# Multi-head maxima of two heads in two matmuls with padded keys; routing positions and gates in eight steps between latent maxima

## The chip, the cores and the metric

The kernel runs on one core of a Trainium2 chip. The metric is the device time of one execution in microseconds (us). The engines are named PE (TensorE), DVE (VectorE), ACT (ScalarE), POOL (GpSimd) and SP (SyncE, which issues most DMAs).

## What is computed

Eight sequences (B = 8) of 256 tokens with 256 channels go through two branches and come together at the end:

```python
xn = _layernorm(x)
s = latent_attention(xn)        # 16 heads, 64 rotary + 16 other dimensions, causal softmax
h = multi_head_attention(rms(xn, w_ln1))   # 16 heads of 16 dimensions, causal softmax
y = xn + h @ Wo.T
f = y + moe(rms(y, w_ln2))      # 8 experts, top 2 of a router, gates = softmax of the two logits
out = x + s * silu(f)
```

All arithmetic is float32. To come close to it on PE, operands are split into a high part, rounded to float32r (a rounded float32 that PE multiplies in one pass), and the rest; a float32 matmul is run in two passes. The softmax needs each row's maximum before the exponential, and both attentions take it in a matmul of their own.

## The kernel before

**The loop.** `batch(b, first, more)` exists once for each engine and is called for b = 0 to 7; each engine runs its own list of work in order, and semaphores tie the lists together. A batch has four stages on PE. *P2* transposes the maxima of the latent scores and then, in eight units of four 128x128 transposes, the multi-head queries (even units) and keys (odd units) of the batch (`stage_p2`, L716). *T1* computes the transposed latent scores head by head (`scores1`), from which ACT takes exponentials, POOL masks them (`causal`), and PE multiplies them with the values four heads at a time (`values(g)`). After each head `max_head` issues the raw scores of the multi-head attention (`max2`), whose row maxima DVE takes (`stage_m2`, `maxima`, L1397 and L1400). *P1* projects the next batch (`stage_p1`), while DVE and POOL apply the rotary terms. *T2* is T1 with the roles changed: transposed multi-head scores (`scores2`) and, between them, the raw latent scores of the next batch (`max1`), whose maxima DVE takes in `stage_m1`.

**An order written by hand.** Other work is hung between the heads with dictionaries `after`, from the index of a head to a function. On DVE in T1: after head 4 the residual sum of the batch behind (`kept`, xn, L1342), after 5 its statistics, after 7 the copy of the next batch's x (`copy_batch`), after 9 the scaled rows for the router, after 12 the low part of the next x. The router's top two (`top_two`) follow the last head, and its last instruction (`ohb`, L1516) releases PE's second projection of P1, as both use the bank `ps[1]`. In T2: splits of the next batch's queries and keys after 3, 5, 7, 12 and 14, rounding of queries (`rounded`) before the even heads, `positions` of the batch behind after head 1 and `gates` after head 4. On PE in T1: transposes of the batch behind's normalised heads after head 0 (`back`, L621), its output projection after 3, the transposes of the next x after 10 (L645), the router's transposes after 11 and logits after 14. `values(0)` waits for the residual sum (x2d).

**Maxima before.** Two heads share the 128 partitions: `kt2` holds keys in pairs, `qt2` holds the queries of each head alone, with zeros in the other head's 64 partitions. For each head PE multiplies 128 queries with 128 keys and the other 128 queries with all 256 keys, into bank `ps[2 + h % 2]`; it waits until DVE is done with head h - 2. The even heads' halves of the query units are cut by ACT, the odd ones' by DVE (`odd_heads`, L1237), three of them ahead of the normalisation (`normalise`, L1322 and L1327) and one behind it.

**Positions, gates and scatters.** For the tokens of the batch behind, DVE computes their row in each chosen expert's list and the gate values, in chains of small instructions of which each waits for the one before (semaphores pst and gst). The last one signals posd, on which POOL's four indirect DMAs (`scatter_slot`, L515) wait. POOL runs them after its masks of heads 9 to 12 of T2 (`slots_between`); the masks of the next heads stand behind them in its queue, and `values(g)` waits for the masks of its heads.

## Time and profile before

| | us |
|---|---|
| median of 3 runs | 956.92 (955.44 to 962.53) |
| the profiled execution, its time | 958.59 |
| its span, from first to last instruction | 956.9 |

| engine | busy us | share | instructions |
|---|---|---|---|
| PE matmuls | 830.5 | 87% | 6432 |
| PE weight loads | 743.6 | 78% | 6432 |
| DVE | 625.2 | 65% | 2207 |
| ACT | 501.6 | 52% | 1089 |
| POOL | 392.2 | 41% | 538 |

The chain of work that ended last is 67% PE, 10% DVE and 9% DMA. The batches run up to about 660 us; then come the experts. The mean granted clock of PE is 0.935 of 2.4 GHz. Busy times of PE are modelled and overlap: a matmul's start to the start of the next is what it costs in a stream. A row of the timeline may merge several instructions of one kind, with their number (x4); the shape shown is then the first one's.

### The profile page before, as it was taken

Reading aid. Unit: us, or ns where it says so; the run is one execution under the profiler, and the core shown is the slowest. Engines: PE = TensorE matmul, PEld = TensorE weight load, DVE = VectorE, ACT = ScalarE, POOL = GpSimd, SP = SyncE. Lnnn points to the kernel's source line nnn. Section 1 sums busy time; section 2 is a strip of 40 time slices with the busy share of each in tenths; the row PEclk is TensorE's granted clock in tenths of the full one; section 3 lists DMA queues with packets and bytes.
Section 4 is the critical chain, followed back from the end, with each engine's and each line's share of the span. In section 5 each row is a group of like instructions: output and inputs, shape, how many; then the busy total and the mean of one; then the engine's idle time right before and its main releaser. Section 6 shows DMA issues by size and latency. Waiting matters only on the chain.

```text
span 956.9 us, 18123 instructions
## 1 busy us (share of the span) xinstructions
PE 830.5 (87%) x6432; PEld 743.6 (78%) x6432; DVE 625.2 (65%) x2207; ACT 501.6 (52%) x1089; POOL 392.2 (41%) x538
## 2 busy tenths in 40 slices
PE   5889999999999999999998998965269999998980
PEld 3868978978887887887897897843169999998980
DVE  4876677667677667757758757632257777776754
ACT  3445375366366456456356446540146677776651
POOL 5522432343343334344344344331404756555541
PEclk9878999999999999999999999976579999999995
DMA  8000000000000000000000000030236776889736
GB/s 273 1 1 2 13 1 25 12 2 13 24 1 14 13 13 2 24 12 3 23 13 2 24 12 3 23 144 23 47 134 176 221 220 198 238 240 348 193 53 186
DMA packets 39884, 71.04 MB, mean 74 GB/s; under 512 B 10914, under 2 KB 34850, under 8 KB 36834
## 3 DMA queue, kind: packets, MB, share of 16 engines
q1 hardware_dynamic: 29074, 57.39, 17.6%
q0 software_dynamic: 9856, 12.13, 6.7%
q8 instruction: 52, 0.85, 0.4%
q10 hardware_dynamic: 864, 0.36, 0.2%
q14 instruction: 38, 0.31, 0.1%
HBM read 55.12 MB, written 14.81 MB: 73 GB/s over the span
## 4 chain that ended last, share of the span: by engine, by line
PE 67%; DVE 10%; DMA 9%; issue 6%; POOL 2%; ACT 2%; SPq 2%; POOLq 0%; DVEq 0%; ACTq 0%
PE ps L586 54%; DMA expert_rows<-yo,slot_of 6%; PE ps L679 6%; PE ps L716 3%; DVE ps L1400 2%; PE ps L612 2%; DVE ps L1397 1%; SPq L425 1%; PE ps L621 1%; DVE qr L1237 1%; DMA w_ukv_raw<-in_w_ukv 1%; DMA raw<-in_w_experts 1%; SPq L441 1%; POOL slots L515 1%; POOL expert_rows L563 1%
## 5 line engine op out<-in xcount | busy, mean ns | idle before, releaser
L523 POOL TENSOR_SCALAR_AFFINE_SELECT ex<-ex 128x256 f32<-128x256 f32 x256 | 107.6, 425 | 246.5 <-ACT ex L1101 245.1
L1101 ACT ACTIVATE ex<-ps 128x384 f32<-128x384 f32 x256 | 125.4, 497 | 118.9 <-PE ps L586 116.8
L586 PE MATMUL ps<-qt,kt 128*128 128x256 f32 (+1 forms) x768 | 164.1, 325 | 8.6 <-ACT ex L1101 4.6
L502 POOL TENSOR_TENSOR tok<-tok,swp 128x256 f32<-128x256 f32 x128 | 97.4, 761 | 114.7 <-DVE swp L1362 113.7
L1397 DVE CUSTOM_DVE_ANT_0 ps<-ps,mask 128x128 f32<-128x128 f32 x256 | 77.4, 302 | 94.9 <-PE ps L586 90.5
L586 PEld LDWEIGHTS ps<-qt,kt 128*128 128x128 f32 x768 | 108.9, 193 | 20.7 <-issue 9.8
L563 POOL DMA_INDIRECT expert_rows<-yo,slot_of x46 | 78.5, 1707 | 110.8 <-DMA expert_rows<-yo,slot_of 55.6
L1400 DVE CUSTOM_DVE_ANT_0 ps<-ps,mask 128x256 f32<-128x256 f32 x256 | 118.9, 465 | 0.0
L1241 DVE TENSOR_TENSOR wel<-raw,weh 128x768 fp32r<-128x768 f32 x92 | 88.4, 961 | 37.2 <-ACT weh L971 36.0
L586 PE MATMUL ps<-wh,xth 128*128 128x320 f32 (+2 forms) x352 | 96.9, 358 | 3.7 <-DVE wl L1241 2.8
L1358 DVE TENSOR_TENSOR tok<-ps,cos_t 128x320 f32<-128x320 f32 x128 | 62.9, 491 | 52.8 <-PE ps L586 52.2
L586 PE MATMUL ps<-xeh,weh 128*128 128x256 f32 x368 | 79.4, 298 | 11.8 <-issue 9.9
L971 ACT ACTIVATE qt<-ps 128x512 f32<-128x512 f32 (+1 forms) x96 | 57.2, 596 | 61.9 <-PE ps L679 59.8
L971 ACT ACTIVATE kt<-ps 128x512 f32<-128x512 f32 (+1 forms) x96 | 57.4, 598 | 53.4 <-PE ps L679 48.3
L586 PE MATMUL ps<-wh,xtl 128*128 128x320 f32 (+2 forms) x352 | 84.1, 321 | 0.0
L586 PE MATMUL ps<-wl,xth 128*128 128x320 f32 (+2 forms) x352 | 83.8, 320 | 0.0
L971 ACT ACTIVATE weh<-raw 128x768 fp32r<-128x768 f32 x92 | 77.9, 846 | 10.1 <-DMA raw<-in_w_experts 10.1
L679 PE MATMUL ps<-idf,tok 128*128 128x128 f32 x512 | 77.0, 273 | 0.0
L586 PE MATMUL ps<-xeh,wel 128*128 128x256 f32 x368 | 75.9, 289 | 0.0
L586 PE MATMUL ps<-xel,weh 128*128 128x256 f32 x368 | 75.8, 288 | 0.0
L586 PE MATMUL ps<-kt,qt 128*128 128x128 f32 (+1 forms) x256 | 73.4, 368 | 0.0
L586 PE MATMUL ps<-kr,qr 128*128 128x128 f32 (+1 forms) x256 | 58.6, 316 | 16.8 <-DVE negm L1400 13.1
(160 smaller groups left out, 1918.3 us busy)
## 6 DMA issues: line engine op xcount, KB each, us to landing
raw<-in_w_experts SPq DMA_DIRECT2D x23, 1536.0 KB
mla_branch<-s_b SPq DMA_DIRECT2D x8, 256.0 KB, 2.1
expert_rows<-xn SPq DMA_DIRECT2D x8, 256.0 KB, 2.2
x_normalised<-otk SPq DMA_DIRECT2D x8, 256.0 KB, 2.1
xr<-in_x SPq DMA_DIRECT2D x1, 2048.0 KB
s_tok<-mla_branch SPq DMA_DIRECT2D x1, 2048.0 KB
w_cols_raw<-in_w_cols SPq DMA_DIRECT2D x1, 1792.0 KB, 15.4
x<-expert_rows SPq DMA_DIRECT2D x3, 512.0 KB, 5.2
```

What stands on the lines that cost most here:

```text
L502: nc.gpsimd.tensor_tensor(t, t, swp[:, n % 2, :, :], ALU.add).then_inc(tokd, 1)
L523: nc.gpsimd.affine_select(a, a, [[0, 2], [1, P]], ALU.is_ge, zero, 0, -1).then_inc(exm, 1)
L563: nc.gpsimd.indirect_dma_start(ys[:, :], bass.IndirectOffsetOnAxis(mt_b[:, blk, j, 1:2], 0), yo[:, blk % 2, j, :], None, compute_op=ALU.ad ...
L586: return nc.tensor.matmul(o, a, m, start=start, stop=stop, skip_group_check=True, **k)
L679: t = nc.tensor.transpose(ps[2 + n % 2][:, j * P:(j + 1) * P], tok[:, n % 4, j, :], idf[:, :])
L716: i = nc.tensor.transpose(bank2(u)[:, j * P:(j + 1) * P], a[:, p0:p0 + P], idf[:, :])
L971: return nc.scalar.activation(o, a, ACT.Copy)
L1101: nc.scalar.activation(ex[:, h % (2 * G), :], ps[4 + h % 2][:, P:4 * P], ACT.Exp, scale=scale).then_inc(ex_, 1)
L1241: return nc.vector.tensor_tensor(o, a, b.bitcast(F32), ALU.subtract)
L1358: nc.vector.tensor_tensor(tok[:, n % 4, :, 0:HW], a, cos_t[:, tt:tt + 1, :].broadcast_to([P, G, HW]), ALU.mult)
L1397: nc.vector.tensor_tensor_reduce(out=o[:, 0:P], in0=o[:, 0:P], in1=mask2[:, 1, :], scale=-1.0, scalar=-2.0 * BIG, op0=ALU.add, op1=ALU.min ...
L1400: nc.vector.tensor_tensor_reduce(out=o[:, S:2 * S], in0=o[:, S:2 * S], in1=mask2[:, :, :].rearrange("p a k -> p (a k)"), scale=-1.0, scala ...
```

## The change

`qt2` now holds queries in pairs and `kt2` the keys of each head alone, padded with zeros. A pair of heads has its maxima in two matmuls: 128 queries against the first 128 keys of both heads (256 columns, bank `ps[3]`), and the other 128 queries against all keys of both (512 columns, bank `ps[2]`). PE issues them after every second head, each one when DVE is done with the same bank of the pair before. DVE takes two maxima of 128 columns, then two of 256; a function hung after index 4 now runs after the first half of pair 2. The odd halves are cut from the key units instead of the query units. `scores2` takes the padded keys as weights; its shapes are the same. `positions` and `gates` are cut into eight steps; in batches 1 to 6 they are hung after the latent maxima of heads 1, 2, 4, 6, 8 (two steps), 9 and 10, and elsewhere they run as before. The four scatters move from behind the masks of heads 9 to 12 to behind those of heads 11 to 14, the last batch's too. The memory cleared by POOL is now that of `kt2`.

```diff
@@ -173,8 +173,8 @@
         mask2 = sb("mask2", [P, 2, P], BF16, late)
         wo1 = sb("wo1", [P, ET, E], F32, late)
         wo2 = sb("wo2", [P, ET, E], F32, late)
-        qt2 = sb("qt2", [P, H, S], F32R, late)
-        kt2 = sb("kt2", [P, H // 2, S], F32R, late)
+        qt2 = sb("qt2", [P, H // 2, S], F32R, late)
+        kt2 = sb("kt2", [P, H, S], F32R, late)
         v2 = sb("v2", [P, 2, H, PADV], F32, late)
         ex = sb("ex", [P, 2 * G, 3 * P], F32, late)
         ov = sb("ov", [P, NG, S], F32, late)
...
@@ -385,7 +385,7 @@
                 sp.wait_ge(mte2, b + 1)
                 for e in range(2):
                     r = ST * e + MROW2
-                    sp.dma_start(qt2[r:r + 1, e:H:2, :].bitcast(F32),
+                    sp.dma_start(qt2[r:r + 1, :, :].bitcast(F32),
                                  mt[e * H // 2:(e + 1) * H // 2, :]).then_inc(md2, 16)
 
...
@@ -524,7 +524,7 @@
                     after.get(h, lambda: None)()
 
             def slots_between(r):
-                return {9 + 2 * t + k: lambda t=t, k=k: scatter_slot(r, t, k) for t in range(2) for k in range(2)}
+                return {11 + 2 * t + k: lambda t=t, k=k: scatter_slot(r, t, k) for t in range(2) for k in range(2)}
 
             zero = nc.gpsimd.to_reg(0.0)
@@ -708,7 +708,7 @@
                     if u >= 3:
 
                         wait(pe, t2e, 8 * b + u - 2)
-                        if (u - 3) % 2 == 0:
+                        if (u - 3) % 2 == 1:
                             wait(pe, t2o, 4 * b + (u - 3) // 2 + 1)
                     a = (qs, ks)[u % 2][:, u // 4, :, :].rearrange("p h c -> p (h c)").bitcast(F32)
                     for j in range(4):
@@ -737,12 +737,20 @@
 
             def max2(b):
                 def head(h):
-                    if h == 0:
+                    if h % 2 == 0:
+                        return
+                    j = h // 2
+                    if j == 0:
                         wait(pe, t2e, 8 * b + 8)
                         wait(pe, t2o, 4 * b + 4)
-                    if h >= 2:
-                        wait(pe, mx2, 16 * b + h - 1)
-                    raw_scores(ps[2 + h % 2], qt2[:, h, :], kt2[:, h // 2, :]).then_inc(m2d, 1)
+                    else:
+                        wait(pe, mx2, 16 * b + 2 * j - 1)
+                    mm(ps[3][:, 0:2 * P].rearrange("p (e k) -> p e k", e=2), qt2[:, j, 0:P],
+                       kt2[:, 2 * j:2 * j + 2, 0:P], True, True).then_inc(m2d, 1)
+                    if j > 0:
+                        wait(pe, mx2, 16 * b + 2 * j)
+                    mm(ps[2][:, :].rearrange("p (e k) -> p e k", e=2), qt2[:, j, P:S],
+                       kt2[:, 2 * j:2 * j + 2, :], True, True).then_inc(m2d, 1)
                 return head
 
@@ -782,8 +790,8 @@
                 return mm(o[:, 2 * P:4 * P], kt[:, h, 0:P], qt[:, h, :], True, True)
 
             def scores2(h, o):
-                mm(o[:, 0:2 * P], kt2[:, h // 2, P:S], qt2[:, h, :], True, True)
-                return mm(o[:, 2 * P:4 * P], kt2[:, h // 2, 0:P], qt2[:, h, :], True, True)
+                mm(o[:, 0:2 * P], kt2[:, h, P:S], qt2[:, h // 2, :], True, True)
+                return mm(o[:, 2 * P:4 * P], kt2[:, h, 0:P], qt2[:, h // 2, :], True, True)
 
             def stage_t1(b, after):
@@ -1075,11 +1083,11 @@
                     t = slice(u // 4 * P, (u // 4 + 1) * P)
                     a = bank2(u)[:, :].rearrange("p (h t) -> p h t", h=4)
                     if u % 2 == 0:
+                        copy(qt2[:, 4 * (u // 2 % 2):4 * (u // 2 % 2) + 4, t], a).then_inc(t2e, 1)
+                    else:
 
                         h0 = 8 * (u // 2 % 2)
-                        copy(qt2[0:ST, h0:h0 + 8:2, t], a[0:ST, :, :]).then_inc(t2e, 1)
-                    else:
-                        copy(kt2[:, 4 * (u // 2 % 2):4 * (u // 2 % 2) + 4, t], a).then_inc(t2e, 1)
+                        copy(kt2[0:ST, h0:h0 + 8:2, t], a[0:ST, :, :]).then_inc(t2e, 1)
                     after.get(u, lambda: None)()
 
@@ -1387,9 +1395,18 @@
 
             def stage_m2(b, after):
                 wait(dve, mtr2, b)
-                for h in range(H):
-                    maxima(b, h, (h % 2) * (H // 2) + h // 2, negm2, m2d, mx2)
-                    after.get(h, lambda: None)()
+                for j in range(H // 2):
+                    for t in range(2):
+                        wait(dve, m2d, 16 * b + 2 * j + t + 1)
+                        n = (t + 1) * P
+                        for e in range(2):
+                            o = ps[3 - t][:, e * n:(e + 1) * n]
+                            col = e * (H // 2) + j
+                            i = nc.vector.tensor_tensor_reduce(
+                                out=o, in0=o, in1=mask2[:, 1 - t:2, :].rearrange("p a k -> p (a k)"), scale=-1.0,
+                                scalar=-2.0 * BIG, op0=ALU.add, op1=ALU.min, accum_out=negm2[:, t, col:col + 1])
+                        i.then_inc(mx2, 1)
+                        after.get(2 * j + t, lambda: None)()
 
@@ -1419,11 +1436,11 @@
 
             def odd_heads(b, i):
 
-                wait(dve, tr2, 8 * b + 2 * i + 1)
+                wait(dve, tr2, 8 * b + 2 * i + 2)
                 t = slice(i // 2 * P, (i // 2 + 1) * P)
                 h0 = 8 * (i % 2)
-                copy(qt2[ST:P, h0 + 1:h0 + 8:2, t],
-                     bank2(2 * i)[ST:P, :].rearrange("p (h t) -> p h t", h=4)).then_inc(t2o, 1)
+                copy(kt2[ST:P, h0 + 1:h0 + 8:2, t],
+                     bank2(2 * i + 1)[ST:P, :].rearrange("p (h t) -> p h t", h=4)).then_inc(t2o, 1)
 
@@ -1451,8 +1468,10 @@
                                      14: lambda: rounded(b + 1, 1)})
                     after = splits(b + 1)
                     if not first:
-                        after[1] = lambda: positions(b - 1)
-                        after[4] = lambda: gates(b - 1)
+                        in_expert, chosen, summed, kept, stepped = position_steps(b - 1)
+                        plus_one, inverse, both = gate_steps(b - 1)
+                        after |= {1: in_expert, 2: chosen, 4: summed, 6: kept, 8: lambda: (stepped(), plus_one()),
+                                  9: inverse, 10: both}
                     stage_m1(b + 1, after)
...
+            def position_steps(r):
+
+                def in_expert():
+                    dve.wait_ge(rnk, r + 1)
+                    nc.vector.tensor_tensor(pose[:, :, :], ps[1][:, 0:2 * NE].rearrange("p (t e) -> p t e", t=2),
+                                            base[:, :].unsqueeze(1).broadcast_to([P, 2, NE]), ALU.add).then_inc(pst, 1)
+
+                def chosen():
+                    dve.wait_ge(pst, 6 * r + 2)
+                    nc.vector.tensor_tensor(base[:, :], ps[1][:, 2 * NE:3 * NE], base[:, :], ALU.add).then_inc(pst, 1)
+                    for t in range(2):
+                        i = nc.vector.tensor_tensor(posx[:, t, :, :], oh[:, t, :, :],
+                                                    pose[:, t:t + 1, :].broadcast_to([P, 2, NE]), ALU.mult)
+                    i.then_inc(pst, 1)
+
+                def summed():
+                    dve.wait_ge(pst, 6 * r + 4)
+                    nc.vector.tensor_reduce(posf[:, :, :].rearrange("p t k -> p (t k)"),
+                                            posx[:, :, :, :].rearrange("p t k e -> p (t k) e"), AX.X,
+                                            ALU.add).then_inc(pst, 1)
+
+                def kept():
+                    dve.wait_ge(pst, 6 * r + 5)
+                    wait(dve, msc, 64 * r)
+                    copy(posu[:, :, :], posf[:, :, :])
+                    ids = rc[:, C_IDS:C_IDS + 8].rearrange("p (t k f) -> p t k f", t=2, k=2)
+                    for t in range(2):
+                        i = copy(meta[:, t, :, 0:2], ids[:, t, :, :])
+                    i.then_inc(pst, 1)
+
+                def stepped():
+                    dve.wait_ge(pst, 6 * r + 6)
+                    step = rc[:, C_IDS:C_IDS + 8].rearrange("p (a f) -> p a f", f=2)
+                    nc.vector.tensor_scalar(step[:, :, :], step[:, :, :], 2.0 * P, None, ALU.add).then_inc(gst, 1)
+                return in_expert, chosen, summed, kept, stepped
+
+            def gate_steps(r):
+                g = meta[:, :, :, 2].bitcast(F32)
+
+                def plus_one():
+                    dve.wait_ge(gex, r + 1)
+                    nc.vector.tensor_scalar(gsum[:, :], gexp[:, :], 1.0, None, ALU.add).then_inc(gst, 1)
+
+                def inverse():
+                    dve.wait_ge(gst, 3 * r + 2)
+                    nc.vector.reciprocal(gsum[:, :], gsum[:, :]).then_inc(gst, 1)
+
+                def both():
+                    dve.wait_ge(gst, 3 * r + 3)
+                    copy(g[:, :, 0], gsum[:, :])
+                    nc.vector.tensor_tensor(g[:, :, 1], gexp[:, :], gsum[:, :], ALU.mult).then_inc(posd, 1)
+                return plus_one, inverse, both
+
             def positions(r):
...
```

## Rows read from the trace of the kernel before

**Rows 1.** Windows, four stages of a batch: stretch, length, busy us, granted clock, DMA

```profile
core 0: us, PE busy (x) PEld busy (x) DVE busy (x) ACT busy (x) POOL busy (x), PEclk, DMA share, GB/s
370.20:375.00 4.80, 4.79 (x42) 4.50 (x43) 2.60 (x6) 3.71 (x9) 0.00 (x0) 1.00 0.03 7
375.00:396.50 21.50, 21.27 (x174) 18.37 (x173) 15.08 (x75) 11.42 (x26) 7.25 (x17) 1.00 0.08 26
396.50:425.00 28.50, 28.36 (x219) 26.88 (x218) 17.38 (x53) 12.00 (x23) 11.95 (x16) 1.00 0.04 12
425.00:444.70 19.70, 16.90 (x154) 12.80 (x151) 16.75 (x91) 13.03 (x32) 10.84 (x20) 1.00 0.01 1
```

**Rows 2.** Timeline of PE in T1: start, us, tiles, shapes, count, idle before

```profile
377.05 0.82 PE L586 MATMUL ps<-qt,kt 128*128 128x128 f32 x4
...
377.93 0.82 PE L586 MATMUL ps<-qt,kt 128*128 128x128 f32 x4
```

**Rows 3.** Timeline of PE in T2: scores and maxima, then a projection

```profile
432.23 0.39 PE L586 MATMUL ps<-kr,qr 128*128 128x128 f32 x2
432.46 0.40 PE L586 MATMUL ps<-qt,kt 128*128 128x256 f32 x2
432.69 0.39 PE L586 MATMUL ps<-kr,qr 128*128 128x128 f32 x2
...
436.31 0.63 PE L586 MATMUL ps<-wl,xth 128*128 128x512 f32 x2
436.77 0.63 PE L586 MATMUL ps<-wh,xtl 128*128 128x512 f32 x2
```

**Rows 4.** Timeline from P2 into T1

```profile
374.12 0.60 PE L716 MATMUL ps<-idf,qs 128*128 128x128 f32 x4
...
374.57 0.63 PE L716 MATMUL ps<-idf,ks 128*128 128x128 f32 x4
...
375.67 0.42 PEld L621 LDWEIGHTS ps<-idf,otk 128*128 128x128 f32 x4 [0.22 <-DVE otk L1327]
```

**Rows 5.** Timeline of T1, heads 4 to 6

```profile
382.51 0.30 DVE L1397 CUSTOM_DVE_ANT_0 ps<-ps,mask 128x128 f32<-128x128 f32 x1
...
382.72 0.47 DVE L1400 CUSTOM_DVE_ANT_0 ps<-ps,mask 128x256 f32<-128x256 f32 x1
...
383.10 0.69 DVE L1342 TENSOR_TENSOR xn<-ps,xn 128x512 f32<-128x512 f32 x1
...
384.17 0.59 PEld L586 LDWEIGHTS ps<-ex,v 128*32 128x32 f32 x16
```

**Rows 6.** Timeline at the start of P1, second projection

```profile
398.86 0.30 PEld L586 LDWEIGHTS ps<-wh,xth 128*128 128x128 f32 x2 [0.43 <-DVE ohb L1516]
```

**Rows 7.** Timeline of DVE and PE in the front of T2

```profile
427.79 0.17 DVE L1521 TENSOR_TENSOR pose<-ps,base 128x16 f32<-128x16 f32 x1
...
429.10 0.41 DVE L1237 CAST qr<-qt 128x512 fp32r<-128x512 f32 x1
...
430.31 0.47 PE L586 MATMUL ps<-kr,qr 128*128 128x128 f32 x2 [1.12 <-DVE negm L1400]
```

**Rows 8.** Timeline of POOL, ACT and PE at the end of T2

```profile
439.73 0.98 POOL L515 DMA_INDIRECT slots<-meta,posu  x1 [0.17 <-issue]
...
441.35 0.98 POOL L515 DMA_INDIRECT slots<-meta,posu  x1 [0.17 <-issue]
442.35 1.13 POOL L523 TENSOR_SCALAR_AFFINE_SELECT ex<-ex 128x256 f32<-128x256 f32 x3
...
437.67 0.49 ACT L1101 ACTIVATE ex<-ps 128x384 f32<-128x384 f32 x1 [0.76 <-PE ps L586]
...
443.53 0.86 PE L586 MATMUL ps<-ex,v 128*32 128x256 f32 x16
444.72 0.39 PE L602 MATMUL ps<-idf,negm 128*16 128x128 f32 x2 [0.34 <-DVE negm L1400]
```

**Rows 9.** Windows around a fall of the granted clock, T2 of another batch

```profile
350.73:354.15 3.42, 2.15 (x13) 1.49 (x12) 3.28 (x23) 3.23 (x9) 1.91 (x5) 1.00 0.00 0
354.15:357.56 3.41, 3.30 (x15) 3.33 (x16) 2.35 (x15) 0.00 (x0) 0.29 (x1) 0.50 0.03 5
```

38 lines of the change are left out of this document (6 added, 32 removed).

## The prediction

> **What bounds the kernel now.** I read the page first: TensorE (PE) is busy most of the span, and two thirds of the chain that ended last is PE. So any PE time that is saved counts, and so does any new wait in PE's in-order queue. Then I cut one batch of the steady state into its four stages and took the windows of each [rows 1]: 4.8 us of transposes (P2), 21.5 us of latent scores with the multi-head maxima between them (T1), 28.5 us of projections (P1), 19.7 us of multi-head scores with the latent maxima (T2). T1 and P1 are PE-bound (21.27 of 21.50 us busy). T2 is not (16.90 of 19.70): there PE, VectorE (DVE) and GpSimd (POOL) wait for each other. A batch is 74.5 us, and six of the eight (1 to 6) are alike; the figures below are for one of these.
>
> **The maxima on PE.** In T1 a head of latent scores and a head of maxima together take 0.88 us from start to start [rows 2]. The old maxima of a head (128 columns, then 256) take 0.23 us, exactly what two matmuls of 256 columns take; in both cases 0.115 us each, so 128 columns cost as much as 256 [rows 3]. A matmul of 512 columns of the same kind takes 0.23 us: two of them 0.46 us. So a pair of heads cost 4 x 0.115 = 0.46 us and will cost 0.115 + 0.23 = 0.35 us: 0.11 us saved per pair, 0.9 us per batch, 7 us in all if PE never waits. Scores alone are 0.88 - 0.23 = 0.65 us. The price of the new forms is the least certain in the first term: nothing saved (0.46) at one end, 0.33 at the other.
>
> The Trainium skill (TensorE: Matmul & The Clock Gate, "Back-to-back issue gap") gives N/2.4 + 2.5 ns for an isolated matmul: 56, 109 and 216 ns for 128, 256 and 512 columns, so 330 ns a pair before and 325 after. The trace disagrees in the first of these: 115 ns for the 128 columns. By the rule the change saves PE nothing.
>
> **What becomes late because of it.** DVE needs 0.21 us from the start of a 128-column maximum to the next instruction and 0.38 us for a 256-column one [rows 5]: 0.6 us a head, 1.2 us a pair, far below PE's 1.65 us. But both heads now wait for one issue, behind the scores of the next head, and what DVE does between maxima waits with them. I walk PE through P2 and T1.
> (a) P2. The odd halves are now cut from keys, whose transposes come one unit after the queries'. A unit is 0.45 us of PE [rows 4]. DVE's third odd copy stands ahead of the normalisation (reciprocals, two products), and PE's weights for the transposes of its result already waited 0.22 us for it [rows 4]. So these come 0.45 us later, and head 1 with them: +0.46 us.
> (b) The residual sum of the batch behind (xn, 0.69 us) runs after the first maxima of pair 2 instead of after head 4. DVE began head 4's maxima at 382.51 [rows 5], 0.43 after their issue (0.23 of matmul, 0.2 of passing on), so the scores of head 6 ended one head later, at 382.96. Pair 2 is issued there: +0.46 - 5 x 0.23 + 2 x 0.35 = +0.01, at 382.97. Then 0.12 of matmul, 0.2 to DVE, 2 x 0.21, 0.69 for xn, 0.05 back: 384.45. The first values wait for xn; they started at 384.17 [rows 5], and PE would be there at 384.0. So +0.3 us instead of -0.1.
> (c) Pair 3 and the batch copy behind it slip the same way (statistics, 1.34 us, stand between): the transposes of the next x start some 0.6 us late, and half of that is regained up to head 12. At head 13 I have +0.47. The router's logits wait for a ScalarE copy that follows head 13, so pair 6 gains nothing.
> (d) End of T1. The last issue comes 0.23 us earlier (head 14's maxima are no longer before the values), but DVE then has 2 x 0.21 + 2 x 0.38 = 1.20 us to do behind it, not 0.60, less 0.12 since it starts after one matmul: +0.25. PE already waits there for the marked experts that follow the maxima [rows 6], so it lands in full: +0.7 us at the start of P1. P1 is PE-bound and carries it on.
>
> **Positions and gates.** Eight steps spread over T2. Before, the positions held DVE from 427.79 to 429.10: 1.31 us between two maxima, mostly one small instruction waiting for the one before; PE stood idle 1.12 us for the maxima behind them [rows 7]. Now one step (0.08 us) stands there, so the next maxima come 1.2 us earlier and PE with them. The other steps (about 0.08 us each when nothing is waited for, 10 instructions) are added where DVE was continuously busy, heads 6 to 9: -0.2. At head 11 I have -1.05 us. The gates cost nothing before (PE was in a projection) and 0.25 us now, in that sum.
>
> **The scatters behind them.** They are ready only after head 10, so the four scatters move on POOL from behind the masks of heads 9 to 12 to behind those of heads 11 to 14. A mask is 0.42 us, a scatter 0.98 us, from one scatter to the next with the mask and the gaps 1.62 us [rows 8]. Before, the last mask ended at 443.48 and the values of the last group started at once (443.53); only 0.34 us of slack lay between them and the next stage, which waited for DVE [rows 8]. Now: exp of head 11 ends at 438.16 - 1.05 = 437.1, its mask at 437.6, first scatter 437.8 to 438.8; the mask of head 12 at 439.06 (its exp binds), then three times 1.62 and a mask: 444.35. The last values start at 444.4, 0.88 us, P2 at 445.28 instead of 444.72: **+0.56 us** where the shorter DVE chain alone would have given -1. What is queued behind the masks on POOL is only the next batch's; what waits for them is PE, and with it everything.
>
> **The clock.** In three of the six batches (one is shown, the two others look the same) the granted clock fell to 0.50 (1.2 GHz) for 3.4 us after the front of T2; in the 3.42 us before, PE had 13 matmuls and 2.15 us busy [rows 9]. I take a fall there at 1.5 us: 3.3 us of PE work at half clock, less what was waiting anyway. The front gets denser, so I take these off: -4.5 us. But PE now stands idle some 2.5 us before the last values (last maxima done near 441.8, values at 444.4), a thinner stretch than the one shown. I expect falls there in four to six batches, each doubling the values and transposes after it for part of the time: 1.3 us each, +6.5. Net +2, bounds -4.5 (no fall) and +5.
>
> **Sum.** Batches 1 to 6: 6 x (0.7 + 0.56) = +7.6. Batch 0 has no residual sum, router or scatters: -0.6. The last batch: T1 +0.7, and its scatters, in a T2 where POOL is busy throughout, +0.3. Together +8.0, with the clock +10. The profiled execution has a span of 956.9 us in a time of 958.6; its span happens to equal the median, so the forecast is 956.9 + 10 = **967 us**.
>
> **Rivals.**
> 1. *Slower by waits and POOL, as worked out:* 962 to 974 us, with the clock deciding where. Chance 0.62.
> 2. *The same waits, but no falls of the clock at the end of T2, or half of the slips taken up by slack I did not see:* 3 to 4 us over, 957 to 962. For it: PE's waits in T1 are each only 0.3 to 0.5 us. Chance 0.22.
> 3. *Faster: the scatters do not hold PE.* It decides at a scatter's hold on POOL of under about 0.65 us; then P2 comes 1 us earlier: 6 x (0.7 - 1.0) - 0.6 + 0.7 - 4.5 = -6, 951 us. Against it: all four are 0.98 to 1.03 us, and the old last mask already ended 0.06 us before its values. Chance 0.07.
> 4. *PE saves nothing by the wider matmuls* (512 columns dearer than in the projections, 0.46 us a pair): +0.11 x 6 pairs more per batch, about 972 us. Chance 0.05.
> 5. *The clock, once fallen at the end of T2, stays low through P2,* whose 42 matmuls are nearly all transposes. At half clock a transpose takes twice its 0.11 us, so 4.4 us per batch: 8 - 4.5 + 26, near 987 us. Against it: P2 shows a clock of 1.00 throughout [rows 1]. Chance 0.04.
>
> Rival 5 is what the Trainium skill says (same page, "PE-mode transpose"): transposes don't count as busy in the same way and don't bring the full clock. By that rule P2 should have lost it; the trace does not agree so far, but shows no P2 that began low.
>
> **Numbers.** Changes of 1% (9.6 us, the bounds 947.4 and 966.5) are about what a measurement of this kernel can tell from none. Slower by over 1%: most of the upper half of rival 1, rivals 4 and 5: 0.47. Within: lower half of rival 1, rival 2: 0.47. Faster: part of rival 3: 0.06. The range 956 to 974 leaves out rivals 3 and 5.
>
> **What would show it.** Right: two matmuls in place of four, in 0.35 us a pair, in T1; idle on PE before its transposes of the normalised heads and before the first values, naming xn; no 1.1 us idle for the maxima in the front of T2; the last mask about 0.9 us later than before counted from the stage's start, and PE's last values released by POOL after over 2 us idle; the clock at 0.50 in several P2 stages. Wrong: P2 starting under 19.7 us after T2's start, or T1 under 21.5 us.

## The result, and the profile after

| | before | after |
|---|---|---|
| median of four runs each, same chip, us | 956.18 (954.51 to 962.53) | 975.2 (970.45 to 976.21) |
| the profiled execution, us | 958.59 | 975.67 |
| its span, us | 956.9 | 973.9 |
| mean granted clock | 0.935 | 0.935 |

The changed kernel takes 1.0177 times as long (95% interval 1.0119 to 1.0234), 17 us more by this ratio and by the two spans (the medians stand 19 us apart). It is slower, on the side that was forecast, and 8 us beyond the single number.

Windows of the kernel after. The first three are P2, T1 and P1 of a steady batch, the fourth a T2 without a fall of the clock (another batch), the last two the stretch before the end of a T2 and the one after it. They answer to [rows 1, 9]; as there, the windows part T1 from P1 at the first projection.

```profile
core 0: us, PE busy (x) PEld busy (x) DVE busy (x) ACT busy (x) POOL busy (x), PEclk, DMA share, GB/s
453.17:458.05 4.88, 4.81 (x46) 4.53 (x43) 2.08 (x3) 3.95 (x9) 0.00 (x0) 1.00 0.04 7
458.05:480.30 22.25, 21.08 (x158) 16.68 (x157) 14.75 (x74) 11.58 (x26) 7.25 (x17) 1.00 0.07 25
480.30:509.10 28.80, 28.27 (x217) 26.74 (x216) 17.99 (x57) 11.79 (x23) 11.94 (x16) 1.00 0.03 11
587.10:607.47 20.37, 17.10 (x154) 12.90 (x153) 16.29 (x91) 12.76 (x31) 10.96 (x20) 1.00 0.02 2
527.00:529.00 2.00, 0.26 (x7) 0.17 (x10) 0.80 (x5) 0.00 (x0) 1.50 (x3) 1.00 0.03 2
529.00:532.40 3.40, 3.40 (x28) 2.72 (x21) 0.00 (x0) 1.35 (x3) 0.00 (x0) 0.50 0.02 4
```

P2 takes 4.88 us for 4.80, T1 22.25 for 21.50, P1 28.80 for 28.50, T2 20.37 for 19.70. PE's busy time fell in T1 (21.08 for 21.27), but its idle time rose by more. The last two rows are the fall that the forecast looked for: 0.26 us of PE in the 2 us before, then 3.4 us at 0.50, and 1.00 again behind it.

Timeline of PE in T1, in the start of P1 and at the end of a T2, kernel after (start, us, engine, line, operation, tiles, shapes, count, idle before it and what ended that). It answers to [rows 4, 5, 6, 8].

```profile
459.29 0.66 PE L621 MATMUL ps<-idf,otk 128*128 128x128 f32 x4 [0.41 <-DVE otk L1335]
...
467.77 0.86 PE L586 MATMUL ps<-ex,v 128*32 128x256 f32 x16 [0.39 <-DVE xn L1350]
...
477.33 1.06 PE L586 MATMUL ps<-wr,s_b 128*128 128x8 f32 x8 [0.27 <-ACT s_b L979]
...
483.00 0.56 PE L586 MATMUL ps<-wh,xth 128*128 128x320 f32 x2 [0.53 <-DVE ohb L1535]
...
513.41 0.47 PE L586 MATMUL ps<-kr,qr 128*128 128x128 f32 x2
...
528.75 1.32 PE L586 MATMUL ps<-ex,v 128*32 128x256 f32 x16 [2.57 <-POOL ex L523]
530.00 0.59 PE L602 MATMUL ps<-idf,negm 128*16 128x128 f32 x2
```

The longest waits of PE are ones that the forecast had named: its transposes of the normalised heads (0.41 us for DVE's product), the first values (0.39 us for xn), the second projection of P1 (0.53 us behind the transposes, for ohb), and 2.57 us for POOL before the last values, where the kernel before had its masks done in time [rows 8]. The 1.12 us of idle time in the front of T2 [rows 7] are gone; the matmul that stood behind them starts at 513.41 without a wait. The next P2 begins at 530.00, although DVE was done with the last latent maxima at 527.8. DVE's rows of the first step (pose), of the last (meta) and of the last maxima, same T2, with [rows 7, 8] of before:

```profile
511.93 0.17 DVE L1541 TENSOR_TENSOR pose<-ps,base 128x16 f32<-128x16 f32 x1
...
521.90 0.16 DVE L1587 TENSOR_TENSOR meta<-gexp,gsum 128x2 f32<-128x2 f32 x1
...
527.67 0.13 DVE L1417 DVE_READ_ACCUMULATOR2_ANT negm<- 128x1 f32 x1
```

The last step, which signals posd, ends at 522.1. POOL, same T2:

```profile
522.34 1.03 POOL L515 DMA_INDIRECT slots<-meta,posu  x1 [0.38 <-DVE meta L1587]
...
524.13 0.97 POOL L515 DMA_INDIRECT slots<-meta,posu  x1 [0.17 <-issue]
...
527.28 0.97 POOL L515 DMA_INDIRECT slots<-meta,posu  x1 [0.17 <-issue]
528.28 0.41 POOL L523 TENSOR_SCALAR_AFFINE_SELECT ex<-ex 128x256 f32<-128x256 f32 x1
```

Each scatter waits behind a mask and each mask behind a scatter, 1.57 to 1.79 us apart. The last mask ends at 528.7, 19.57 us after T2's start at 509.12; before, it was 18.49 us (443.48 - 424.99).

**Where the 17 us are.** The table adds up stages from the starts of PE's instructions (P2 begins with the transposes of the latent maxima, T1 with the first latent score, P1 here with the transposes of the multi-head maxima, 1.8 us later than in the windows, T2 with the first multi-head score). Each value is that of a batch without a fall in the stage or running into it; batches 1 to 6 agree within 0.03 us, but for one T2 of the kernel before (20.11).

| us | P2 | T1 | P1 | T2 |
|---|---|---|---|---|
| before | 4.82 | 23.31 | 26.65 | 19.74 |
| after | 4.88 | 24.01 | 27.06 | 20.36 |

That is 1.79 us a batch, 10.7 us in six. From the start of batch 1's P2 to that of batch 7's it is 452.5 us before and 464.3 after, 11.8 more; so the falls in between cost 1.1 us more than before. The last batch adds 4.9 us: 1.7 in a P2 with a fall, 1.3 in T1, 1.9 in T2 (up to the transposes of its values). Batch 0 and what is ahead of it add 0.1, the experts 0.2.

### The profile page after: what moved, and what is told of

It is laid out like the page before. It is cut to its first block, busy times and chain, and to the rows that moved or that the text cites. A ratio compares the mean times of both kernels' runs of the same rounds, so it can differ in the third digit from the quotient of the medians.

```text
span 973.9 us, 17859 instructions
## 1 busy us (share of the span) xinstructions
PE 831.5 (85%) x6304; PEld 730.8 (75%) x6304; DVE 619.4 (64%) x2207; ACT 501.1 (51%) x1089; POOL 393.6 (40%) x538
## 4 chain that ended last, share of the span: by engine, by line
PE 55%; DMA 14%; issue 11%; DVE 8%; POOL 7%; ACT 4%; SPq 0%; POOLq 0%; ACTq 0%; DVEq 0%
PE ps L586 42%; DMA expert_rows<-yo,slot_of 11%; PE ps L679 6%; POOL slots L515 3%; PE ps L716 3%; PE ps L612 2%; ACT ex L1109 1%; POOL ex L523 1%; POOL expert_rows L563 1%; DVE ps L1405 1%; PE ps L621 1%; POOL xg L552 1%; DMA w_ukv_raw<-in_w_ukv 1%; DMA xg<-x_normalised,slot_of 1%; DVE otk L1335 1%
## 5 line engine op out<-in xcount | busy, mean ns | idle before, releaser
L586 PE MATMUL ps<-qt,kt 128*128 128x256 f32 (+1 forms) x768 | 159.1, 326 | 6.0 <-issue 3.2
L586 PEld LDWEIGHTS ps<-qt,kt 128*128 128x128 f32 x768 | 113.6, 193 | 21.0 <-ACT ex L1109 7.6
L1405 DVE CUSTOM_DVE_ANT_0 ps<-ps,mask 128x128 f32<-128x128 f32 (+1 forms) x256 | 85.0, 384 | 57.1 <-PE ps L586 57.0
L586 PE MATMUL ps<-xeh,weh 128*128 128x256 f32 x368 | 78.6, 296 | 11.8 <-issue 9.8
L586 PE MATMUL ps<-ex,v 128*32 128x256 f32 (+1 forms) x1024 | 57.5, 344 | 22.5 <-POOL ex L523 19.8
L1196 ACT ACTIVATE sg<-ps 128x256 f32<-128x256 f32 x92 | 35.7, 388 | 69.3 <-PE ps L586 66.6
L586 PEld LDWEIGHTS ps<-xeh,weh 128*128 128x128 f32 x368 | 57.9, 195 | 15.8 <-issue 15.8
```

Of the source, the lines that this page charges most:

```text
L586: return nc.tensor.matmul(o, a, m, start=start, stop=stop, skip_group_check=True, **k)
L1196: nc.scalar.activation(sg[:, n % 2, :], ps[n % 3][:, 0:BS], ACT.Silu).then_inc(sgd, 1)
L1405: i = nc.vector.tensor_tensor_reduce(out=o, in0=o, in1=mask2[:, 1 - t:2, :].rearrange("p a k -> p (a k)"), scale=-1.0, scalar=-2.0 * BIG, ...
```

## The experiments

There are twelve runs of ten kernels, on four chips; every ratio is against the kernel before on the same chip. Stages are read as in the table above. The part of a run from the last batch's last values on (mostly the experts) took between 301.9 and 307.2 us in the profiled executions, with no relation to the edits, so that stages tell more than spans do.

### Each half alone

The first kernel has the eight steps and the new places of the scatters, nothing of the pairs (the functions of the steps, as in the change, are left out here):

```diff
-                return {9 + 2 * t + k: lambda t=t, k=k: scatter_slot(r, t, k) for t in range(2) for k in range(2)}
+                return {11 + 2 * t + k: lambda t=t, k=k: scatter_slot(r, t, k) for t in range(2) for k in range(2)}
...
-                        after[1] = lambda: positions(b - 1)
-                        after[4] = lambda: gates(b - 1)
+                        in_expert, chosen, summed, kept, stepped = position_steps(b - 1)
+                        plus_one, inverse, both = gate_steps(b - 1)
+                        after |= {1: in_expert, 2: chosen, 4: summed, 6: kept, 8: lambda: (stepped(), plus_one()),
+                                  9: inverse, 10: both}
```

> The kernel before with the second half of the change alone: positions and gates in eight steps, scatters behind the masks of heads 11 to 14; the maxima stay one head at a time. Theory (the two halves cost about the same, and this one costs through GpSimd): the front of T2 gets its 1.05 us back, but the last mask ends with the scatters, so that T2 of batches 1 to 6 is some 0.6 us longer than before when the clock is full, 6 x 0.6 = 3.6 us, the last batch 1.9 (what the changed kernel shows), and the falls of the clock move from the front of T2 to its end, +2.7: 965 us, PE idle over 2 us for POOL before the last values. Rival (T2 became longer because of the padded keys or the order of the maxima, not by the scatters): this kernel has no cause to be slower, and wins 1.05 us per batch and the three falls in front: 945 to 957 us.

Measured: 963.56 us, ratio 1.0113 (1.0076 to 1.0150). Window of a T2 without a fall, and PE's last values in it:

```profile
428.67:449.04 20.37, 17.09 (x154) 12.91 (x153) 16.28 (x91) 12.77 (x31) 10.96 (x20) 1.00 0.01 1
```

```profile
448.25 0.86 PE L586 MATMUL ps<-ex,v 128*32 128x256 f32 x16 [2.58 <-POOL ex L523]
```

T2 is 20.37 us as in the whole change, T1 and P1 are those of the kernel before (23.30 and 26.65). Falls came at the end of T2 or the start of the next P2 in five of the batches 1 to 6, none in the front of T2. So the longer T2 belongs to this half alone, and POOL ends it (2.58 us of idle PE). The profiled span was 960.1 us, 5 below the expectation: the part behind the batches took 4.3 us less than in the kernel before, and the last batch's T2 grew by 0.7 us, not 1.9.

The second has the pairs and nothing of the steps:

```diff
-                    raw_scores(ps[2 + h % 2], qt2[:, h, :], kt2[:, h // 2, :]).then_inc(m2d, 1)
+                    mm(ps[3][:, 0:2 * P].rearrange("p (e k) -> p e k", e=2), qt2[:, j, 0:P],
+                       kt2[:, 2 * j:2 * j + 2, 0:P], True, True).then_inc(m2d, 1)
+                    if j > 0:
+                        wait(pe, mx2, 16 * b + 2 * j)
+                    mm(ps[2][:, :].rearrange("p (e k) -> p e k", e=2), qt2[:, j, P:S],
+                       kt2[:, 2 * j:2 * j + 2, :], True, True).then_inc(m2d, 1)
```

> The kernel before with the first half alone: maxima of two heads in two matmuls, odd halves cut from keys; positions, gates and scatters as before. Theory: PE starts the second projection of P1 1.1 us later per batch than before (+0.7 in T1, +0.4 behind it), 6 x 1.15 = 7 us, the last batch 1.3, batch 0 0.2: about 965 us, with T2 and its falls of the clock as before (19.74 us without a fall). Rival (the delay in T1 comes from what the second half leaves behind, falls of the clock at the end of T2 and transposes at a low clock): T1 23.3 us and no more than 958 us.

Measured: 959.99 us, ratio 1.0058 (1.0031 to 1.0085); its profiled span 965.3 us. T1 24.01, P1 27.04, and T2 as before, with the three falls in its front, as before. The window of a T2 without a fall, and PE's second projection of P1:

```profile
505.00:524.68 19.68, 16.87 (x155) 12.84 (x152) 16.90 (x91) 12.76 (x31) 10.60 (x20) 1.00 0.01 2
```

```profile
403.21 0.56 PE L586 MATMUL ps<-wh,xth 128*128 128x320 f32 x2 [0.53 <-DVE ohb L1533]
```

The same 0.53 us for ohb as in the whole change. So the two halves hit different stages, and their ratios multiply to that of the whole (1.0113 x 1.0058 = 1.0172). The stages of the rival stated with this run did not appear: this half costs its 1.1 us a batch without any fall at the end of T2.

### Do the scatters hold T2, and does their wait let the clock fall?

```diff
             def slots_between(r):
-                return {11 + 2 * t + k: lambda t=t, k=k: scatter_slot(r, t, k) for t in range(2) for k in range(2)}
+                return {H - 1: lambda: [scatter_slot(r, t, k) for t in range(2) for k in range(2)]}
```

> The changed kernel with all four scatters behind the mask of head 15, where POOL has nothing to do until the first mask of the next T1 some 6 us later. Theory (the last values wait for POOL's masks, which stand behind the scatters, and the clock falls in this wait): the last mask follows its exponential at about 17.4 us of T2, the last values start there, and the next P2 waits only for the last latent maxima, which end at 527.8 where P2 now starts at 530.0: 2.1 us less in each of six batches, 1.5 in the last, and no fall of the clock at the end of T2 (8.2 us): 973.9 - 12.6 - 1.5 - 8.2 = 951.6 us of span. Rival (the falls at the end of T2 come from its thin stretch whatever waits there, since PE still waits a little for the masks): the falls stay and only the waits go, about 960 us. Rival (the maxima on DVE set the end of T2, and the scatters just fill the time): under 3 us, 970 us or more.

Measured: 943.24 us, ratio 0.9904 (0.9866 to 0.9942), span 941.6. Windows of P2 and of T2:

```profile
438.20:443.09 4.89, 4.82 (x43) 4.54 (x44) 2.08 (x3) 3.69 (x9) 2.37 (x3) 1.00 0.04 5
494.16:512.39 18.23, 17.07 (x154) 12.88 (x152) 15.83 (x91) 13.13 (x32) 8.37 (x18) 1.00 0.01 1
```

```profile
512.39 0.39 PE L602 MATMUL ps<-idf,negm 128*16 128x128 f32 x2 [0.45 <-DVE negm L1417]
```

T2 fell from 20.36 to 18.23 us, and PE's last wait is again 0.45 us for DVE. Not one fall of the clock is left in batches 1 to 6, neither in the front of T2 nor at its end. From batch 1's P2 to batch 7's it is 445.3 us, for 464.3: 19.0 less, of which 12.8 are waits and the rest falls. So the scatters set the end of T2, and without the 2.6 us of idle PE there was no fall. The span is 10 us below the 951.6 expected: 1.9 of these lie ahead of batch 1, 4.7 behind the batches and 3.5 in the last T2, where the clock was low for a shorter time; the steady batches came as expected. The changed kernel with its scatters out of the way is 1% faster than the kernel before.

The same edit on the kernel before, positions whole:

```diff
-                return {9 + 2 * t + k: lambda t=t, k=k: scatter_slot(r, t, k) for t in range(2) for k in range(2)}
+                return {H - 1: lambda: [scatter_slot(r, t, k) for t in range(2) for k in range(2)]}
```

> The kernel before with one edit: all four scatters behind the mask of head 15 (positions and gates whole, maxima one head at a time). Theory (in the kernel before two things end T2 at nearly the same time, POOL's masks and DVE's latent maxima, which positions held up for 1.3 us in front): taking away the one alone gives next to nothing, T2 without a fall stays at 19.6 to 19.74 us, the falls in the front of T2 stay, 953 to 957 us of span. Rival (the scatters alone bound T2, and the eight steps are worth nothing): T2 at 18.2 us, 6 x 1.5 = 9 us less, 948 us.

Measured: 967.24 us, ratio 1.0102 (1.0061 to 1.0142). Window of the one T2 without a fall, and PE's wait in its front:

```profile
430.64:449.72 19.08, 16.85 (x154) 12.82 (x151) 16.19 (x91) 12.78 (x31) 8.38 (x18) 1.00 0.01 1
```

```profile
435.95 0.47 PE L586 MATMUL ps<-kr,qr 128*128 128x128 f32 x2 [1.11 <-DVE negm L1400]
```

The 1.11 us for the maxima behind the positions are there as in [rows 7]. In the five other batches the clock fell in the front of T2, which then takes 20.65 to 21.05 us; without a fall it is 19.08, by this one batch. Neither the theory (19.6 to 19.74) nor the rival (18.2) had this: of the 1.5 us between 19.74 and 18.23, 0.65 come from the scatters alone, with the positions' hold still there, and 0.85 more with the steps. That the kernel became slower, and not only no faster, is another matter: all its P2 from batch 2 on took 6.7 to 8.1 us, the two longest with a fall of the clock in them. This was not expected, and came in all four kernels that ran on that chip.

### A stall in P2 that depends on the chip or the run

This kernel is the one with the eight steps and without the pairs, and the same line for the scatters.

> The kernel before with positions and gates in eight steps and the scatters behind the mask of head 15; maxima one head at a time. Against the 941.6 us of the changed kernel with the scatters there it differs only in the maxima. Theory (pairs cost 1.1 us per batch at the end of T1 and the start of P1, as maxima alone showed, and save nothing elsewhere): 941.6 - 6 x 1.1 - 1.3 = 934 us, T2 of 18.2 us and no fall of the clock in batches 1 to 6. Rival (with T2 short, the thinner T2 and the denser T1 change where the clock falls): falls in T2 or P2 come back, 1.3 us each, 940 us.

Measured: 953.16 us, ratio 0.9936 (0.9907 to 0.9965). T1 23.30, P1 26.65, T2 18.25 and no fall in batches 1 to 6, all as in the theory, but P2 7.25 us. ACT and PE there (the last copy of values and what follows it):

```profile
442.09 0.38 ACT L971 ACTIVATE ov<-ps 128x256 f32<-128x256 f32 x1 [1.22 <-PE ps L586]
445.14 0.38 ACT L971 ACTIVATE ov<-ps 128x256 f32<-128x256 f32 x1 [2.66 <-remote]
```

```profile
442.06 0.86 PE L586 MATMUL ps<-ex,v 128*32 128x256 f32 x16
...
445.57 1.09 PE L612 MATMUL ps<-idf,ov 128*128 128x128 f32 x8 [1.39 <-issue]
```

PE issued the last values at 442.06, and the copy that waits for them alone began at 445.14, 2.66 us of idle ACT whose end the trace puts down to nothing of this core (remote), while POOL issued its four scatters. In the changed kernel with the scatters last the copy came 0.9 us after the values' issue. ACT is not alone in this: DVE's first odd copy began 3.8 us after PE had issued the transposes that it reads (443.58 to 447.38), and 0.7 us after them in the second run of this kernel below (436.17 to 436.87). So what came late is PE's side of the hand-over, its work or its signals, and not ACT. To see whether kernel or chip makes the difference, both ran again elsewhere:

> The same kernel as the changed one with the scatters last, measured once more beside the two below, because the four kernels with the scatters there that ran on another chip all had a P2 of 6.7 to 7.3 us at full clock, where this one had 4.9: ScalarE's last copy of the values, released by PE's last values, came 2.2 us late. Theory A (four scatters in a row hold up PE's last values as PE's own semaphores show it, and whether they do depends on the chip or the run): here P2 is 6.8 us in at least some batches and the time lies between 943 and 957 us. Theory B (it depends on the kernel's own timing, and this kernel is free of it): P2 is 4.9 us again and the time 943 us.

Measured: 946.73 us, ratio 0.9896 (0.9870 to 0.9923), P2 4.89 (in batches 2 and 3 of both its runs 5.28 to 5.66, most of which T1 made up).

> The kernel before with positions and gates in eight steps and the scatters behind the mask of head 15, once more. In its first run each P2 of batches 2 to 7 held ScalarE's last copy of the values back by 2.2 us and took 6.8 to 7.3 us; the changed kernel with the same scatters has not shown this on two other chips. Theory A (it hangs on the chip or the run): on another chip P2 is 4.8 us in batches 2 to 7 and the span 951.3 - 6 x 2.4 = 937 us. Theory B (it hangs on the kernel: when its last values meet the scatters): P2 is 6.8 to 7.3 us again and the span 951 us.

Measured: 935.95 us, ratio 0.9783 (0.9755 to 0.9811), span 936.9, P2 4.82 but for batch 2 (5.50). The same copy of ACT:

```profile
435.57 0.38 ACT L971 ACTIVATE ov<-ps 128x256 f32<-128x256 f32 x1 [0.84 <-PE ps L586]
```

The same kernel has the stall on one chip and none on another, so theory A holds for it. What makes it is open; no run here separates chip from run. For the comparison it leaves a clean pair, on different chips: with the scatters last and no stall, maxima one head at a time take 935.95 us (ratio 0.978) and pairs 943 to 947 us (0.990 both times). The pairs by themselves cost some 8 us by the stages, 6 x 1.1 and 1.3 in the last T1, and 1.2% by the ratios.

### Why the pairs cost what they do

```diff
                         for e in range(2):
                             o = ps[3 - t][:, e * n:(e + 1) * n]
                             col = e * (H // 2) + j
+                            if t == 1:
+                                o = o[:, P:2 * P]
                             i = nc.vector.tensor_tensor_reduce(
-                                out=o, in0=o, in1=mask2[:, 1 - t:2, :].rearrange("p a k -> p (a k)"), scale=-1.0,
+                                out=o, in0=o, in1=mask2[:, 1, :], scale=-1.0,
```

> The changed kernel, with the 256-column maxima of the second half of a pair taken over their last 128 columns only (so the maximum subtracted is that of the diagonal block): two instructions of 0.21 us in place of two of 0.38 us. It takes 0.34 us of DVE from each pair and nothing from PE. In the changed kernel a pair costs PE 0.40 to 0.48 us where 0.35 was expected: in batch 0 the pairs start at 81.75, 83.52 and 85.21 us, 1.77 and 1.69 us apart, of which two heads of scores are 1.31. Theory (PE's second matmul of a pair waits until DVE is done with the pair before, as its weights are loaded only then): the pairs stand 1.66 us apart, batch 0's T1 is some 0.5 us shorter (18.75 us), and ohb comes 0.7 to 0.9 us earlier in each of batches 1 to 6. Rival (the matmul of 512 columns, or of two strided blocks, is dearer by itself): the distances stay 1.70 or more and batch 0's T1 stays at 19.2 us; only the 0.34 us at the end of T1 are won, about 2 us in all.

Measured: 969.85 us in one run (the kernel before on the same chip: 954.76), so that only its trace is read here. Pairs of batch 0 in T1, first the changed kernel (PE, then its weight loads, then DVE), then the one with short maxima (PE):

```profile
82.29 1.58 PE L586 MATMUL ps<-qt,kt 128*128 128x128 f32 x8
...
84.08 1.47 PE L586 MATMUL ps<-qt,kt 128*128 128x128 f32 x8
...
85.79 0.38 PE L586 MATMUL ps<-qt,kt 128*128 128x128 f32 x2
```

```profile
82.94 0.52 PEld L586 LDWEIGHTS ps<-qt,kt 128*128 128x128 f32 x4 [0.24 <-ACT ex L1109]
```

```profile
82.26 0.30 DVE L1405 CUSTOM_DVE_ANT_0 ps<-ps,mask 128x128 f32<-128x128 f32 x1 [1.58 <-PE ps L586]
...
83.55 0.14 DVE L1405 DVE_READ_ACCUMULATOR2_ANT negm<- 128x1 f32 x1
84.02 0.30 DVE L1405 CUSTOM_DVE_ANT_0 ps<-ps,mask 128x128 f32<-128x128 f32 x1 [0.33 <-PE ps L586]
```

```profile
81.88 1.58 PE L586 MATMUL ps<-qt,kt 128*128 128x128 f32 x8
...
83.64 1.47 PE L586 MATMUL ps<-qt,kt 128*128 128x128 f32 x8
...
85.31 0.82 PE L586 MATMUL ps<-qt,kt 128*128 128x128 f32 x4
```

From one pair of scores to the next it is 1.79 and 1.71 us, and with short maxima 1.76 and 1.67; less two heads of scores (1.31) the second of each is 0.40 and 0.36. In the first, a weight load also waits 0.24 us for ACT's exponential, as two heads of scores now come without maxima between them. DVE begins 0.5 us after the pair's first matmul is issued and needs 1.4 us for its four maxima (82.26 to 83.69), and PE's next second matmul needs that bank: the loop is as long as PE's own. Batch 0's T1 is 18.78 us, the theory's 18.75, against 19.24 in the changed kernel and 19.29 before. So of the 0.9 us that eight pairs should save there, DVE's part of the loop takes 0.46, as this run shows, and 0.05 are left; the rest goes with the wait for the exponentials, which no run took away. In batches 1 to 6 T1 and P1 are 0.27 us shorter each, 0.54 of the 0.7 expected.

### The waits in T1 taken away one by one

```diff
-                odd_heads(b, 2)
                 normalise()
+                odd_heads(b, 2)
                 odd_heads(b, 3)
-                after = {4: kept}
+                after = {1: kept}
                 if not first:
                     after[5] = lambda: stats_x2(b - 1)
                     after[9] = lambda: scale_x2(b - 1)
+                    after[13] = lambda: top_two(b - 1)
...
                 stage_m2(b, after)
-                if not first:
-                    top_two(b - 1)
```

The first of these kernels has only the lines on `top_two`, the second all; both have the scatters last.

> The changed kernel with the scatters last and the router's top two hung behind the second half of pair 6 instead of behind the last pair: they need the logits, which PE finishes near 478.4 us, and DVE sits idle from 478.7 to 480.3. Theory (the last pair's 1.2 us on DVE push the top two, and PE's second projection waits for their last instruction): ohb comes 2 us earlier, PE's second projection follows the transposes of the maxima directly, as in batch 0, T1 unchanged at 24.0, P1 at 26.25: 941.6 - 6 x 0.8 = 937 us. Rival (the top two now stand ahead of the last pair and hold it up, and the transposes of the maxima with it): T1 grows by 0.2 to 0.5 us and half of the gain is lost, 939 to 940 us.

Measured: 954.76 us, ratio 0.9976 (0.9954 to 0.9998), on the chip with the stall (P2 6.75 to 7.07). The junction of T1 and P1:

```profile
472.69 0.39 PE L602 MATMUL ps<-idf,negm 128*16 128x128 f32 x2
472.83 0.54 PE L586 MATMUL ps<-wh,xth 128*128 128x320 f32 x2
```

The 0.53 us are gone, P1 is 26.24 us as in batch 0, T1 still 24.0: the theory's stages. Its time is the stall's. The rival's longer T1 did not come.

> The same with two more moves in DVE's order: the normalisation ahead of the third odd copy, and the residual sum behind pair 0 instead of in the middle of pair 2. Theory (PE's 0.41 us for the transposes of the normalised heads and its 0.39 us for xn before the first values are paid in full): T1 23.2 us, 6 x 0.8 = 4.8 us below the kernel with the top two alone, 932 us. Rival (the time won in front is lost to the next wait, DVE's work on the pair before and ScalarE's copy before the logits): T1 no shorter than 23.6, 935 us or more.

Measured: 947.55 us, ratio 0.9893 (0.9857 to 0.9929), with the stall (P2 6.75 to 7.09, and 8.03 where the clock fell in it). T1 is 22.82 us, 1.2 less than with the top two alone, where 0.8 was expected and the rival had 23.6. The transposes of the normalised heads start 0.65 us into T1, for 1.23 in the changed kernel, the first values 8.62 for 9.71, the logits 18.08 for 19.27: almost all is won at the two waits, which had cost 0.58 and some 0.5 us and not only the 0.41 and 0.39 that PE was idle.

### Scatters one by one in the next T1

The other edits of the kernel with all moves stay.

```diff
             def slots_between(r):
-                return {11 + 2 * t + k: lambda t=t, k=k: scatter_slot(r, t, k) for t in range(2) for k in range(2)}
+                return {H - 1: lambda: [scatter_slot(r, t, k) for t in range(2) for k in range(2)]}
+
+            def slots_t1(b):
+                after = {6: lambda: power2(b - 1)}
+                if b >= 2:
+                    for n, h in enumerate((3, 11, 14, 15)):
+                        after[h] = lambda n=n: scatter_slot(b - 2, n // 2, n % 2)
+                return after
...
-                causal(b, ex1, exm1, {6: lambda: power2(b - 1)})
+                causal(b, ex1, exm1, slots_t1(b))
                 rope_sums(b + 1)
-                causal(b, ex2, exm2, slots_between(b - 1))
+                causal(b, ex2, exm2, {})
```

> The changed kernel with the top two behind pair 6, the normalisation ahead of the third odd copy, the residual sum behind pair 0, and the four scatters of a batch one by one in the next T1, behind the masks of heads 3, 11, 14 and 15, where POOL is idle for 1.6 to 2.3 us each (the last batch keeps its own behind the mask of head 15). Theory (a scatter costs only what stands behind it in POOL's queue, or what four in a row hold up at the start of P2): P2 4.9, T1 22.8, P1 26.2, T2 18.2, so 72.2 us a batch without a fall of the clock, 6 x 2.6 + 5.5 (falls) + 2 (last batch) = 23 us below the kernel before: 933 us of span. Rival (scatters hold up PE wherever they stand): T1 grows by up to 4 x 1 us and the time is 950 us or more.

Measured: **930.77 us, ratio 0.9742 (0.9723 to 0.9760)**, span 928.7: 2.6% faster than the kernel before, and by the two ratios (0.9742 / 1.0177) some 4% faster than the changed one. Windows of one batch, and POOL around its first and its last scatter:

```profile
429.91:434.80 4.89, 4.82 (x43) 4.54 (x44) 2.48 (x6) 3.67 (x9) 0.00 (x0) 1.00 0.01 3
434.80:455.86 21.06, 20.79 (x159) 16.68 (x158) 15.80 (x82) 11.48 (x26) 10.26 (x21) 1.00 0.09 27
455.86:483.86 28.00, 28.00 (x218) 26.78 (x216) 16.74 (x47) 11.78 (x23) 12.90 (x17) 1.00 0.04 11
483.86:502.09 18.23, 17.09 (x155) 12.90 (x152) 15.83 (x91) 13.14 (x32) 6.81 (x16) 1.00 0.01 1
```

```profile
439.53 0.98 POOL L515 DMA_INDIRECT slots<-meta,posu  x1 [0.16 <-issue]
...
455.85 0.97 POOL L515 DMA_INDIRECT slots<-meta,posu  x1 [0.17 <-issue]
```

72.18 us a batch, as expected (72.2), no fall in batches 1 to 6 and no stall. PE is busy 20.79 of 21.06 us in T1 and 28.00 of 28.00 in P1 (the windows part them at the first projection; by the table's cut they are 22.81 and 26.24). Behind each scatter POOL is idle again, 0.43 to 0.85 us for ACT behind the first three and 1.13 us for DVE behind the last. The rival (T1 longer, 950 us) did not come.

The last kernel has the same edits on single heads: the diff of the eight steps, `top_two` behind index 13, `normalise` ahead of the third odd copy, and the scatters as here.

> The kernel before with the same edits and without the pairs: maxima one head at a time, positions and gates in eight steps, scatters in the next T1, top two behind the maxima of head 13, normalisation ahead of the third odd copy. Theory (once no wait hangs on a whole pair, the pairs are worth what PE saves by them: 0.46 less 0.40 us a pair, some 0.4 us a batch): T1 23.1 to 23.2 us and P1 26.25, so this kernel is 2 to 3 us slower than the one with pairs. Rival (pairs are still worse): T1 under 22.8 us here.

Measured: 940.21 us, ratio 0.9843 (0.9819 to 0.9867). PE at the end of its P2:

```profile
441.13 0.63 PE L723 MATMUL ps<-idf,ks 128*128 128x128 f32 x4 [0.85 <-DVE qt L1244]
```

T1 23.27, P1 26.25, T2 18.25, and P2 5.83 where 4.82 was meant: here the third odd copy is cut from the bank that the last unit of keys needs, so with the normalisation ahead of it PE waits 0.85 us. That move pays with pairs and costs 1.0 us a batch with single heads. With the P2 of the other kernels (4.82) a batch would be 72.6 us, 0.4 more than with pairs. So the theory's 0.4 us a batch agrees with the stages, but was not measured in one kernel: of the 9.8 us between the two spans some 7 are the new wait.

## Why the prediction was right, and where its sum was not

The forecast was 967 us, with slower by waits and POOL as the likeliest case (962 to 974) and a range up to 974. The median is 975.2, 1 us above the range; the profiled span, from which the sum was made, is 973.9. The cause is that case's: slower, by the waits it names. The sum had 10 us and 17 came, nearly every term too small.

**The maxima on PE: the saving did not come.** 0.35 us a pair was expected; 0.40 and 0.48 came in turn, by the distances in batch 0, where the old maxima took 0.46. The step that failed is that DVE's 1.2 us a pair is "far below PE's 1.65 us". It is not the sum that counts but the loop: the start of DVE 0.5 us behind the issue, 1.4 us of maxima, then the bank. This loop eats half of the gain and the exponentials of two heads in a row, as far as the trace tells, nearly all of the other half. Batch 0 shows it alone: T1 19.24 us for 19.29, where the sum had -0.6 us.

**(a) Normalised heads:** +0.46 expected; from the start of T1 they come 1.23 us (458.06 to 459.29) where it was 0.66 (375.03, the start of T1 in the trace, to 375.69), +0.57, DVE's product named. Right, a tenth short.

**(b) xn and the first values:** +0.3 expected, +0.57 measured (467.77 from the start of T1 at 458.06, for 9.14 in [rows 5]). Pair 2 was issued 0.15 us later than walked, as (a) and the price of two pairs make it; the maxima took 0.05 and xn with its signal 0.09 more than the sum had.

**(c) The middle of T1:** the step that failed is that the slip is 0.6 us at the transposes of the next x and half of it is regained up to head 12. It was 0.92 at these transposes (471.66 from 458.06, for 387.71 from 375.03), 0.70 at the values behind head 12, and 0.82 for 0.47 at the logits, which ACT's copy releases as expected (0.27 us of idle).

**(d) The junction:** +0.7 us expected at the second projection of P1, +1.1 measured. The 0.6 us of DVE behind the last issue are as walked. The other 0.36 are the excess of (c). This is 6 x 0.4 = 2.4 us of the sum; the top two hung between pairs took the whole wait away.

**Positions:** the matmul that waited 1.12 us [rows 7] starts 4.29 us into T2 (513.41 - 509.12), for 5.32 before (430.31 - 424.99): -1.03, with -1.2 expected there and -1.05 further on. Right.

**Scatters:** first at 13.22 us of T2, last mask ending at 19.57, T2 20.36 for 19.74: +0.62 where +0.56 stood. Right, and shown by three kernels: without the pairs (20.37), with the scatters last (18.23), and in T1 (18.24).

**The clock:** -4.5 for the fronts and +6.5 for four to six falls at the end were expected. The fronts had none, the ends five (in batches 1, 2, 3, 5 and 6, each running into the next P2), for 8.2 us; before, three cost 5.1, and one T2 was 0.4 us longer without a fall. Net +2.7, +2 expected, which is near in part by luck: the fronts gave back 1.0 us more than expected and the ends cost 1.7 more. What a fall at the end costs was 1.6 us, not 1.3.

**The last batch:** +1.0 expected, +3.2 without its P2's fall. T1 grew by 1.3 us: the 0.8 us of slip at the logits, and 0.45 us more that PE waits for DVE's last maxima, since here no projection lies between the last pair and the transposes of the maxima. In T2 the steps and scatters alone cost 0.7 us (positions alone), and the rest goes with the clock, 0.53 for 14.4 us there:

```profile
640.90:655.30 14.40, 11.47 (x57) 9.21 (x57) 4.13 (x19) 5.00 (x11) 2.85 (x7) 0.53 0.53 217
```

In the kernel before 0.55 lasted 11.4 us. The pairs alone show a longer one too (17.1 us at 0.50). But this part need not come from the edit: in two runs of one and the same kernel (changed, scatters last) the clock of the last batch was at 0.50 for 10.2 and for 17.1 us, and its T2 took 21.36 and 22.38 us up to the last values. No run decides it.

**Rivals.** Rival 5, a clock that stays low through P2, did not come: five times the clock fell just before or just after P2's start and was at 1.00 again 3.4 us after the fall. In batch 4 nothing but transposes ran at 0.50 (its P2 began at 375.19, and the first latent score behind it came at 381.75):

```profile
375.40:378.80 3.40, 3.40 (x18) 3.40 (x17) 0.00 (x0) 1.24 (x3) 0.00 (x0) 0.50 0.02 5
378.80:381.70 2.90, 2.83 (x26) 2.57 (x25) 2.05 (x3) 2.65 (x6) 0.00 (x0) 1.00 0.00 0
```

The Trainium skill (TensorE: Matmul & The Clock Gate, "PE-mode transpose") says that transposes don't bring the full rate; by that rule P2 should have stayed low, and the trace disagrees. Rival 4 (0.46 us a pair, dearer matmuls) has nearly the size of what came, but not the cause: with short maxima the same matmuls come at 0.36 us a pair. Rival 3 asked for a hold of under 0.65 us, and a scatter held POOL for 0.97 to 1.03 us. The side that it stood for is there all the same: with POOL free at the end of T2 the changed kernel takes 943 us. The 7 us that the sum lacks are 6 x 0.53 = 3.2 in P2, T1, P1 and T2 of the steady batches, 0.7 in batch 0, 0.6 in the last T1, 1.6 in the last T2, 0.7 of clock and 0.2 in the experts.

## What to carry to other kernels

A saving on the engine that bounds a stage is worth its wait loop: before two small pieces are merged, walk the loop issue, consumer, buffer free with the consumer's whole batch, and look at what hangs behind it in the consumer's queue. Work that sits on a shared in-order queue (scatters behind masks) belongs in stretches where that engine waits for others, one piece at a time; ask of each engine where its longest idle waits are, also in the next stage. When two engines end a stage within a fraction of a microsecond of each other, an edit to one of them shows only part of its worth until the other is moved too, so try them together before judging either.
